# Where the inverse square roots of twelve normalisations are computed: eleven VectorE instructions or one GpSimd power

## The chip, the cores and the metric

The kernel runs on one core of a Trainium2 chip. The core has five engines, each with an instruction queue of its own that it works through strictly in order: TensorE (PE in the profile; PEld is its weight load), VectorE (DVE), ScalarE (ACT), GpSimd (POOL) and SyncE (SP, which here only starts DMAs). Engines wait for each other through semaphores. The metric is the device time of one execution in microseconds (us), the median of several runs; less is better.

## What is computed

Two transformer layers on `x` of 2 x 512 tokens with 256 features. What matters here are the normalisations, each of which needs `1/sqrt(v)` of a few numbers for every token:

```
def rmsnorm(x, w, eps=1e-05):
    return x * rsqrt(mean(x * x, axis=-1) + eps) * w
...
# layer 0: layer norm, then an RMS norm of it, feed a gated linear attention (GLA)
S = S * exp(gt) + kt * vt            # 512 steps, a scan over the tokens
ot = einsum('bhk,bhkd->bhd', qt, S)
o = (o - mean(o)) * rsqrt(var(o) + 1e-05)   # per token and head, 16 heads
x = x + (silu(g) * o) @ Wo
x = x + (silu(xn2 @ W1) * (xn2 @ W3)) @ W2  # xn2 = rmsnorm(x): a SwiGLU MLP
# beside it, a ternary-weight MLP on the layer-normed x
h = silu(gate) * up;  h = h * rsqrt(mean(h * h) + eps);  y = h @ Wp
# layer 1: softmax attention, then rmsnorm, a router and a mixture of 8 experts
```

## The kernel before, in words

The tokens are two chunks `c` = 0, 1 of 512 tokens; a chunk is four tiles (TPC = 4) of 128 tokens on the 128 partitions. So the inverse roots of one chunk are a block of 128 partitions x 4 numbers (`ff`, `rms`, `xm`), x 8 (`norm`, `ln`: two norms at once) or x 64 (`gn`: 4 tiles x 16 heads). They all live in the small tile `small`.

The twelve places, in order of time: `norm` of chunk 0 and 1 (prologue), `ff` 0 (norm of the ternary MLP's hidden row), `gn` 0 (norm of the GLA output), `rms` 0, `ff` 1, `gn` 1, `rms` 1, `ln` 0, `ln` 1 (layer 1's first norms) and `xm` 0, `xm` 1 (norm ahead of the router). In the kernel before, all are made by VectorE in `rsqrt`: `rsqrt_guess` (L1529, L1530: a shift and a subtraction on the number's bits) and three Newton rounds (L1535, L1536, L1538), eleven instructions, each waiting for the one before through `link`.

Each engine runs the same written-out list of steps, `order_of(engine)`: a PROLOGUE, then steps put into numbered slots, sorted by slot and by a rank within the slot, then ORDER. A step of which an engine has no part is skipped by it. LATE moves a kind of step one slot later on one engine; RANK says which kinds come first in a slot, and what is not in RANK comes last in the order in which it was put. Slots 0 to 31 carry the 32 GLA steps: PE replicates (`rep`), DVE multiplies (`upd`, L1690) and scans (`scan`, L1698), POOL multiplies with q (`read`, L2192), PE sums (`red`). Between them lie the ternary MLP (`in`, `hm` (DVE L1670; POOL sums the squares into `acc`, L2182), `out`), the group norm of chunk 0 in four stages (`gn`, c, 0 to 3) and its projection (`got`, `wo`). From slot 35 the SwiGLU MLP runs (`hm`: DVE L1670, ACT `ah`, POOL `al` L2174), and beside it the group norm of chunk 1 and the splitting of the next weights in POOL (`w`: `w3l`, `w2l`; `qkvw`). Then come the layer-1 projections, the softmax attention over 64 heads (DVE takes row maxima, L1828) and the experts.

The consumers of the inverse roots: `ff_out` adds the ternary MLP's result to `X` (L1681) and so frees the PSUM banks that PE's `out` of the other chunk waits for; `group_norm` stage 3 scales `cen` (L1730); `rms_scale` (L1750) and `ln2_rows` (L1761) scale `XA`; `norm_rows` (L1577 on DVE, L2159 on POOL) normalises `X`.

Of the kernel before, what the change touches and what calls it, by code (L numbers as in the profile page):

```python
# [30 lines left out]
P = 128  # L31
# [17 lines left out]
RSQRT_SEED = float(0x5F3759DF)  # L49
# [57 lines left out]
def build(nc, orders, w_pack, t_pack, c_pack, r_pack, e_pack, vec_pack, bias_pack, x_in, out):  # L107
    from contextlib import ExitStack
    ctx = ExitStack()
    with ctx:  # L110
# [58 lines left out]
        ah_at = mlp_at + (2 + 3) * CH * 4  # L169
        QSX = at("QSX", [6, CH], F32, ah_at)  # L170
# [149 lines left out]
        factors = tally("norm_factors")  # L320
# [22 lines left out]
        sqr = tally("hidden_square")  # L343
        accr = tally("square_sum")
# [105 lines left out]
        PROLOGUE += [("z", 0), ("norm", 1, "guess")] + pj(0, 3) + [("e1", 0), ("norm", 1, "newton")] + low_at(0, 3) + pj(0, 4)  # L450
# [45 lines left out]
        put(22, ("ss", 0))  # L496
        put(34, ("ss", 1))
# [11 lines left out]
        for n in range(4):  # L509
# [6 lines left out]
        put(32, ("rms", 0, 0))  # L516
# [5 lines left out]
                [("wo", 1, 0)], [("wo", 1, 1)], [("rms", 1, 0)], [("xat", 1, 0)], [("xat", 1, 1)],  # L522
# [5 lines left out]
        for i, s in enumerate(SWS):  # L528
# [7 lines left out]
        LATE = {"PE": {}, "ACT": {"hm": 1}, "POOL": {"hm": 1, "read": 1},  # L536
                "DVE": {"upd": 1, "scan": 1, "tern": 1, "hm": 1, "tr": 1, "proj": 1, "otok": 1, "wo": 1, "ss": 1, "got": 1, "xat": 1}}
        RANK = {"PE": ("rep", "in", "tern", "red", "out"), "ACT": ("in", "hm", "ternA"),
                "POOL": ("read", "tern", "hm"), "DVE": ("tern0", "hm", "upd", "tern", "scan")}
# [261 lines left out]
        def _(pe):  # L801
# [713 lines left out]
        def _(dve):  # L1515
# [11 lines left out]
            def rsqrt_guess(y_, v, n, tmp):  # L1527
                t_ = small[:, tmp, 0:n]
                link(nc.vector.tensor_single_scalar(t_.bitcast(I32), v.bitcast(I32), 1, ALU.logical_shift_right))  # L1529
                link(nc.vector.tensor_scalar(y_.bitcast(I32), t_.bitcast(I32), -1.0, RSQRT_SEED, ALU.mult, ALU.add))  # L1530

            def newton(y_, v, n, tmp, times, told_by=None):
                t_ = small[:, tmp, 0:n]
                for i in range(times):
                    link(nc.vector.scalar_tensor_tensor(t_, y_, -0.5, v, ALU.mult, ALU.mult))  # L1535
                    link(nc.vector.tensor_tensor(t_, t_, y_, ALU.mult))  # L1536
                    last = told_by if told_by and i == times - 1 else link
                    last(nc.vector.scalar_tensor_tensor(y_, t_, 1.5, y_, ALU.add, ALU.mult))  # L1538
# [14 lines left out]
            def norm_stats(layer, c, part=None):  # L1553
# [3 lines left out]
                v, r = small[:, 0, 0:2 * TPC], small[:, 1, 0:2 * TPC]  # L1557
# [7 lines left out]
                if part is None:  # L1565
                    newton(r, v, 2 * TPC, 4, 2)
                elif part == "newton":
                    newton(r, v, 2 * TPC, 4, 2, lambda ins: ins.then_inc(*factors.tick(c)))
                    dve.wait_ge(*factors.upto(c))

            def norm_rows(layer, c):
                r1, r2 = small[:, 1, 0:TPC], small[:, 1, TPC:2 * TPC]
                rows = [("xt", XN, r1), ("x1", XA, r2)]
                for v, dst, r in (rows if layer == 1 else rows[::-1]):
# [131 lines left out]
            def group_norm(c, stage):  # L1706
# [16 lines left out]
                elif stage == 1:  # L1723
                    dve.wait_ge(*g_sq.upto(c))
                    link(nc.vector.tensor_reduce(sm.rearrange("p (t h) -> p t h", h=H), byh(L0["otok"]), AX.X, ALU.add))
                    link(nc.vector.tensor_scalar(vr, sm, 1.0 / HD, EPS, ALU.mult, ALU.add))
                elif stage == 2:
                    rsqrt(rs_, vr, 64, 4)
                else:
# [6 lines left out]
            def rms_factors(half):  # L1736

                v, r = small[:, 0, 0:TPC], small[:, 1, 0:TPC]
                if half == 1:
                    link(nc.vector.tensor_tensor(v, mv[:, :, 0], mv[:, :, 0], ALU.mult))  # L1740
                    link(nc.vector.scalar_tensor_tensor(v, v, EPS, mv[:, :, 1], ALU.add, ALU.add))
                    rsqrt_guess(r, v, TPC, 4)
                    newton(r, v, TPC, 4, 1)
                else:
# [643 lines left out]
```

## Time and profile before

| | us |
|---|---|
| median of 3 runs | 693.27 |
| the three runs | 693.71, 693.27, 685.2 |
| span of the profiled execution (first to last instruction) | 690.8 |
| time of that execution itself | not listed apart; the median run is 2.47 above the span |
| busy: PE, DVE, ACT, POOL | 569.0, 495.7, 302.9, 216.2 |
| GpSimd instructions | 225 |

The span is shorter than a run because a run also holds what lies before the first and after the last instruction. Busy time is an average over stages with different limits, so it does not say which engine a stage waits for.

### The profile page before, as it was taken

Reading aid. Unit: us, or ns where it says so; the run is one execution under the profiler, and the core shown is the slowest. Engines: PE = TensorE matmul, PEld = TensorE weight load, DVE = VectorE, ACT = ScalarE, POOL = GpSimd, SP = SyncE. Lnnn points to the kernel's source line nnn. Section 1 sums busy time; section 2 is a strip of 40 time slices with the busy share of each in tenths; the row PEclk is TensorE's granted clock in tenths of the full one; section 3 lists DMA queues with packets and bytes.
Section 4 is the critical chain, followed back from the end, with each engine's and each line's share of the span. In section 5 each row is a group of like instructions: output and inputs, shape, how many; then the busy total and the mean of one; then the engine's idle time right before and its main releaser. Section 6 shows DMA issues by size and latency. Waiting matters only on the chain.

```text
span 690.8 us, 10947 instructions
## 1 busy us (share of the span) xinstructions
PE 569.0 (82%) x3674; PEld 407.0 (59%) x3678; DVE 495.7 (72%) x1078; ACT 302.9 (44%) x554; POOL 216.2 (31%) x225
## 2 busy tenths in 40 slices
PE   2677689679577799997599988988978889999990
PEld 1544357468356588883255554454535478888870
DVE  5799976997795576858488778768771467767753
ACT  1645433213221223552266545544535656666640
POOL 2765556436545223665200010010044011121120
PEclk9889999989789899996599999999988999999995
DMA  6122000000321004599873431500025794000005
GB/s 185 61 87 75 29 0 1 1 0 1 87 62 30 2 1 133 94 222 284 148 126 69 87 70 24 95 2 2 2 67 234 263 371 138 23 25 32 24 32 190
DMA packets 32733, 58.36 MB, mean 84 GB/s; under 512 B 6822, under 2 KB 24646, under 8 KB 30118
## 3 DMA queue, kind: packets, MB, share of 16 engines
q1 hardware_dynamic: 30422, 52.32, 28.1%
q0 software_dynamic: 1872, 5.13, 2.1%
q8 instruction: 31, 0.51, 0.3%
q10 hardware_dynamic: 384, 0.20, 0.1%
q14 instruction: 24, 0.20, 0.1%
HBM read 41.84 MB, written 15.51 MB: 83 GB/s over the span
## 4 chain that ended last, share of the span: by engine, by line
PE 40%; DVE 11%; issue 3%; POOL 2%; ACT 2%; DMA 1%; SPq 0%; ACTq 0%; POOLq 0%; DVEq 0%
PE bank L823 19%; DVE small L1828 5%; PE bank L1087 5%; PE bank L1064 4%; PE bank L1037 4%; PE bank L817 4%; PE bank L1039 2%; PE bank L1066 1%; DMA yt<-results 1%; PE bank L1104 1%; POOL P3c L2259 1%; POOL rt L2203 1%; ACT PTa L1367 1%; DVE XA L1857 1%; POOL P L2259 1%
## 5 line engine op out<-in xcount | busy, mean ns | idle before, releaser
L1828 DVE TENSOR_REDUCE small<-bank 128x1 f32<-128x256 f32 (+3 forms) x256 | 107.5, 482 | 15.4 <-PE bank L1039 14.2
L1037 PE MATMUL bank<-Ks,Qs 96*128 96x256 bf16 (+3 forms) x256 | 66.6, 327 | 8.6 <-DVE small L1828 7.0
L2104 DVE TENSOR_TENSOR wl<-wall,wh 128x1024 fp32r<-128x1024 f32 x46 | 56.2, 1222 | 22.3 <-ACT wh L1496 21.0
L1064 PE MATMUL bank<-Qs,Ks 99*128 99x512 bf16 (+3 forms) x256 | 60.3, 312 | 8.2 <-issue 7.8
L1367 ACT ACTIVATE PTa<-bank 128x512 f32<-128x512 f32 (+1 forms) x96 | 43.5, 530 | 34.9 <-PE bank L1066 27.2
L1367 ACT ACTIVATE PTb<-bank 128x512 f32<-128x512 f32 (+1 forms) x96 | 43.9, 530 | 27.9 <-PE bank L1066 27.4
L1064 PEld LDWEIGHTS bank<-Qs,Ks 99*128 99x128 bf16 x256 | 25.7, 100 | 51.1 <-issue 32.1
L1039 PE MATMUL bank<-maskb,identb 128*128 128x128 bf16 x256 | 55.4, 234 | 0.0
L1318 ACT ACTIVATE sg<-bank 128x512 f32<-128x512 f32 (+1 forms) x28 | 16.7, 597 | 75.3 <-PE bank L823 75.3
L1496 ACT CAST wh<-wall 128x1024 fp32r x46 | 48.0, 1044 | 2.0 <-issue 0.9
L1066 PE MATMUL bank<-identb,maskb 128*128 128x128 bf16 x256 | 48.2, 226 | 0.0
L2192 POOL TENSOR_TENSOR QSX<-QT,S 128x512 f32<-128x512 f32 x24 | 31.3, 1304 | 41.8 <-DVE S L1698 38.9
L823 PE MATMUL bank<-wall,hT 128*128 x184 | 43.5, 379 | 0.8 <-ACT hT L1511 0.8
L2266 POOL TENSOR_TENSOR X<-X,XA 128x1024 f32<-128x1024 f32 x2 | 4.7, 2366 | 122.3 <-DVE XA L1868 122.3
L1037 PEld LDWEIGHTS bank<-Ks,Qs 96*128 96x128 bf16 x256 | 25.9, 103 | 28.7 <-DVE small L1828 22.4
L1698 DVE TENSOR_TENSOR_SCAN S<-AT,bank 128x512 f32<-128x512 f32 x32 | 38.9, 1215 | 0.6
L823 PEld LDWEIGHTS bank<-wall,hT 128*128 128x128 f32 x184 | 34.7, 189 | 6.3 <-issue 1.0
L823 PE MATMUL bank<-wh,xh 128*128 128x512 f32 x92 | 38.2, 415 | 0.0
L823 PE MATMUL bank<-wpr,hm 128*128 128x256 f32 x128 | 32.5, 399 | 6.6 <-DVE X L1681 6.6
L823 PE MATMUL bank<-wl,xh 128*128 128x512 f32 x92 | 36.2, 393 | 0.0
L823 PE MATMUL bank<-wh,xl 128*128 128x512 f32 x92 | 35.8, 389 | 0.0
L1670 DVE TENSOR_TENSOR hm<-sg,bank 128x512 f32<-128x512 f32 (+1 forms) x28 | 19.1, 682 | 21.6 <-PE bank L823 21.3
(363 smaller groups left out, 1531.7 us busy)
## 6 DMA issues: line engine op xcount, KB each, us to landing
wall<-e_pack SPq DMA_DIRECT2D x8, 1536.0 KB, 8.6
Qs<-pieces SPq DMA_DIRECT2D x48, 128.0 KB, 5.8
stg<-w_pack SPq DMA_DIRECT2D x18, 256.0 KB, 2.8
pieces<-P SPq DMA_DIRECT2D x9, 512.0 KB, 8.5
wf<-t_pack SPq DMA_DIRECT2D x12, 256.0 KB, 2.7
Ks<-pieces SPq DMA_DIRECT2D x8, 384.0 KB, 5.2
sorted_rows<-blank SPq DMA_DIRECT2D x1, 2944.0 KB, 12.7
Ks<-pieces SPq DMA_DIRECT2D x8, 256.0 KB, 4.5
```

The costliest lines, as they stand in the source:

```text
L823: last = nc.tensor.matmul(outap, a, b_, start=start and i == 0, stop=stop and i == n - 1, **kw)
L1037: nc.tensor.matmul(banks[b][:, o:o + w], Q[0:96, h, i * P:(i + 1) * P], K[0:96, h, 0:w], start=True, stop=False)
L1039: last = nc.tensor.matmul(banks[b][:, o + w - P:o + w], identb[:], maskb[:], start=False, stop=True)
L1064: nc.tensor.matmul(banks[b][:, o:o + w], K[0:99, h, j * P:(j + 1) * P], Q[0:99, h, j * P:CH], start=True, stop=False)
L1066: last = nc.tensor.matmul(banks[b][:, o:o + P], maskb[:], identb[:], start=False, stop=True)
L1087: last = nc.tensor.matmul(banks[6][32 * hh:32 * hh + 17, j * P:CH], L1[f"Va{a}"][:, c * TPC + j, 4 * (q % 4) + hh, :], pt[:, hh, PT_AT[j]: ...
L1367: nc.scalar.activation(pt[:, g % 4, lo_:lo_ + w], banks[b][:, 0:w], ACT.Exp).then_inc(*ex.tick((g, i_)))
L1496: nc.scalar.copy(weight_part("h", i, half), wall[:, bass.ds(place + half * KC * EI, KC * EI)])\
L1698: nc.vector.tensor_tensor_scan(L0["S"][:, i % 2, :], L0["AT"][:, c * CH:(c + 1) * CH], banks[i % 2][:], 0.0, ALU.mult, ALU.add).then_inc(* ...
L1828: last = nc.vector.tensor_reduce(mxv[:, i, h:h + 1], banks[b][:, o:o + w], AX.X, ALU.max, negate=True)
L2104: nc.vector.tensor_tensor(weight_part("l", i, half), wall[:, bass.ds(place + half * KC * EI, KC * EI)], weight_part("h", i, half).bitcast( ...
L2192: nc.gpsimd.tensor_tensor(readout(i), L0["QT"][:, c * CH:(c + 1) * CH], L0["S"][:, i % 2, :], ALU.mult).then_inc(*qs.tick(i))
```

## The change

Each of the twelve rounds of eleven VectorE instructions is taken out. VectorE writes the variance and signals it (`var`); GpSimd raises it to the power -0.5 with one two-input instruction, whose second input is one constant read again for every element (`minus_half`), and signals that (`inv`); whoever uses the root waits for `inv`. For `ff` 0, `ff` 1 and `rms` 0, VectorE's variance step gets the rank `first`, so that it comes ahead of the other steps of its slot, and the use stays at the end of the slot. (`gn`, c, 2), once VectorE's eleven instructions, is now GpSimd's power alone. For `norm` 0 of the prologue GpSimd makes the power ahead of its first weight split, for chunk 1 ahead of its `norm_rows`.

```diff
-        put(22, ("ss", 0))
-        put(34, ("ss", 1))
+        put(22, ("ss", 0), ("ssx", 0))
+        put(34, ("ss", 1), ("ssx", 1))
...
-        put(32, ("rms", 0, 0))
+        put(32, ("rms", 0, 0), ("rms", 0, 1))
...
-        LATE = {"PE": {}, "ACT": {"hm": 1}, "POOL": {"hm": 1, "read": 1},
+        LATE = {"PE": {}, "ACT": {"hm": 1}, "POOL": {"hm": 1, "read": 1, "ss": 1},
...
+                if engine == "DVE" and slot < SW_AT and (op == "ss" or it == ("rms", 0, 0)):
+                    op = "first"
...
-            def rsqrt(y_, v, n, tmp):
-
-                rsqrt_guess(y_, v, n, tmp)
-                newton(y_, v, n, tmp, 3)
...
                 if part in (None, "guess"):
                     tell(nc.vector.tensor_scalar(v[:, 0:TPC], mv[:, :, 1], EPS, None, ALU.add))
-                    link(nc.vector.tensor_scalar(v[:, TPC:2 * TPC], mv[:, :, 1], 1.0 + EPS, EPS * EPS, ALU.mult, ALU.add))
-                    rsqrt_guess(r, v, 2 * TPC, 4)
-                    newton(r, v, 2 * TPC, 4, 1)
...
+                    nc.vector.tensor_scalar(v[:, TPC:2 * TPC], mv[:, :, 1], 1.0 + EPS, EPS * EPS, ALU.mult, ALU.add)\
+                        .then_inc(*var.tick(("norm", layer, c)))
...
+            def ff_squares(c):
+                dve.wait_ge(*mm.upto(("ss", c)))
+                nc.vector.tensor_scalar(small[:, 0, 0:TPC], banks[3][:, 0:TPC], 1.0 / 1024, EPS_F32, ALU.mult, ALU.add)\
+                    .then_inc(*var.tick(("ff", c)))
+                dve.wait_ge(*var.upto(("ff", c)))
+
             def ff_out(c):
...
+                dve.wait_ge(*inv.upto(("ff", c)))
...
-                elif stage == 2:
-                    rsqrt(rs_, vr, 64, 4)
-                else:
+                    nc.vector.tensor_scalar(vr, sm, 1.0 / HD, EPS, ALU.mult, ALU.add).then_inc(*var.tick(("gn", c)))
+                    dve.wait_ge(*var.upto(("gn", c)))
+                elif stage == 3:
+                    dve.wait_ge(*inv.upto(("gn", c)))
...
+            nc.gpsimd.memset(minus_half, -0.5).then_inc(*pool_chain.tick(pool_chain.n))
...
+            def inverse_roots(key, dst, src, n):
+
+                pool.wait_ge(*var.upto(key))
+                nc.gpsimd.tensor_tensor(small[:, dst, 0:n], small[:, src, 0:n], minus_half.broadcast_to([P, n]), ALU.pow)\
+                    .then_inc(*inv.tick(key))
+
+            inverse_roots(("norm", 0, 0), 1, 0, 2 * TPC)
...
+                elif op == "ss":
+                    inverse_roots(("ff", it[1]), 1, 0, TPC)
+                elif op == "gn" and it[2] == 2:
+                    inverse_roots(("gn", it[1]), 8, 7, 64)
+                elif op == "rms" and it[2] == 0:
+                    inverse_roots(("rms", it[1]), 1, 0, TPC)
+                elif op == "xm" and it[2] == 1:
+                    inverse_roots(("xm", it[1]), 1, 0, TPC)
+                elif op == "ln" and it[2] == 0:
+                    inverse_roots(("norm", 1, it[1]), 1, 0, 2 * TPC)
```

## Rows read from the trace of the kernel before

**Rows 1.** Windows: stretch, its length, busy PE PEld DVE ACT POOL, PE clock, DMA, GB/s.
```profile
126.00:156.00 30.00, 20.55 (x87) 15.05 (x85) 28.86 (x47) 6.55 (x11) 11.40 (x8) 0.89 0.00 1
156.00:176.00 20.00, 19.89 (x111) 15.41 (x109) 14.78 (x19) 6.84 (x13) 14.96 (x13) 1.00 0.06 15
200.00:225.00 25.00, 17.77 (x101) 15.17 (x102) 17.43 (x26) 6.56 (x11) 12.60 (x12) 0.93 0.08 22
262.00:285.00 23.00, 22.62 (x149) 20.05 (x148) 16.67 (x47) 9.21 (x20) 9.52 (x16) 1.00 0.65 148
```

**Rows 2.** Chain that ended last, attention: start, length, what.
```profile
420.00 1.58 DVE rows L1761 x4
423.94 0.63 PE bank L817 x4
```

**Rows 3.** VectorE's timeline: start, length, line, operation, tiles.
```profile
134.70 1.18 DVE L1535 SCALAR_TENSOR_TENSOR small<-small 128x4 f32<-128x4 f32 x1
...
137.49 1.66 DVE L1681 SCALAR_TENSOR_TENSOR X<-bank,small,X 128x256 f32<-128x256 f32 x4
...
150.98 1.20 DVE L1730 TENSOR_TENSOR cen<-cen,small 128x1024 f32<-128x1024 f32 x1
...
183.92 1.14 DVE L1750 TENSOR_SCALAR cen<-XA,small 128x256 f32<-128x256 f32 x4
...
195.36 1.66 DVE L1681 SCALAR_TENSOR_TENSOR X<-bank,small,X 128x256 f32<-128x256 f32 x4
...
212.22 1.23 DVE L1730 TENSOR_TENSOR cen<-cen,small 128x1024 f32<-128x1024 f32 x1
...
227.59 0.17 DVE L1529 TENSOR_SCALAR small<-small 128x4 int32<-128x4 int32 x1
...
229.77 1.14 DVE L1750 TENSOR_SCALAR cen<-XA,small 128x256 f32<-128x256 f32 x4
...
413.71 0.17 DVE L1529 TENSOR_SCALAR small<-small 128x4 int32<-128x4 int32 x1
...
414.71 1.68 DVE L1828 TENSOR_REDUCE small<-bank 128x1 f32<-128x256 f32 x4
...
417.48 0.18 DVE L1839 CAST mtok<-small 128x16 bf16<-128x16 f32 x1
```

**Rows 4.** GpSimd's timeline: start, length, line, operation, tiles, idle before.
```profile
27.82 4.84 POOL L2159 TENSOR_SCALAR XA<-X,mv,small 128x256 f32<-128x256 f32 x4 [4.82 <-DVE small L1538]
...
134.60 1.26 POOL L2182 TENSOR_TENSOR acc<-acc,sq 128x512 f32<-128x512 f32 x1
...
145.57 1.26 POOL L2182 TENSOR_TENSOR acc<-acc,sq 128x512 f32<-128x512 f32 x1 [0.47 <-ACT sq L1331]
...
180.88 1.00 POOL L2132 TENSOR_TENSOR w3l<-stg,w3h 128x384 fp32r<-128x384 f32 x1
188.88 3.77 POOL L2132 TENSOR_TENSOR w2l<-stg,w2h 128x512 fp32r<-128x512 f32 x3 [6.99 <-ACT w2h L1410]
...
207.02 1.30 POOL L2174 TENSOR_TENSOR al<-hm,ah 128x512 fp32r<-128x512 f32 x1
```

**Rows 5.** VectorE's timeline of the prologue: the last Newton instruction ahead of GpSimd's `norm_rows`.
```profile
27.54 0.17 DVE L1538 SCALAR_TENSOR_TENSOR small<-small 128x8 f32<-128x8 f32 x1
```

**Rows 6.** GpSimd's groups by line and shape: busy us, mean ns of one, idle before.
```profile
L2203 POOL TENSOR_TENSOR rt<-qkt,rope 128x64 f32<-128x64 f32 x16 | 4.4, 294 | 0.0
...
L2142 POOL TENSOR_TENSOR wo1l<-stg,wo1h 128x512 fp32r<-128x512 f32 x1 | 1.3, 1261 | 0.1
...
L2142 POOL TENSOR_TENSOR wrl<-stg,wrh 128x256 fp32r<-128x256 f32 x1 | 0.7, 722 | 0.1
...
L2275 POOL TENSOR_SCALAR rows<-share 128x8 f32<-128x8 f32 x1 | 0.2, 210 | 7.2 <-DMA sorted_rows<-rows,slot_i 7.2
```

**Rows 7.** Waits of the first 36 us: who, for whom, us in total, times, longest.
```profile
PEld bank L817 <- DMA bias<-bias_pack: 10.7, 1, 10.7
```

**Rows 8.** ScalarE's timeline, end of the prologue.
```profile
31.95 0.61 ACT L1309 ACTIVATE ab<-wf 128x512 bf16<-128x512 f32 x1
```

More of the change, by code:

```diff
@@ L169, in build @@
         ah_at = mlp_at + (2 + 3) * CH * 4
+        minus_half = small[:, 11, 63:64]
         QSX = at("QSX", [6, CH], F32, ah_at)
@@ L534, in build @@
         put(SW_AT + SWO_AT[2], ("l1", 0, "xt", 0), ("l1", 0, "xt", 1))
-        LATE = {"PE": {}, "ACT": {"hm": 1}, "POOL": {"hm": 1, "read": 1},
-                "DVE": {"upd": 1, "scan": 1, "tern": 1, "hm": 1, "tr": 1, "proj": 1, "otok": 1, "wo": 1, "ss": 1, "got": 1, "xat": 1}}
+        LATE = {"PE": {}, "ACT": {"hm": 1}, "POOL": {"hm": 1, "read": 1, "ss": 1},
+                "DVE": {"upd": 1, "scan": 1, "tern": 1, "hm": 1, "tr": 1, "proj": 1, "otok": 1, "wo": 1, "ss": 1, "ssx": 1, "got": 1, "xat": 1}}
         RANK = {"PE": ("rep", "in", "tern", "red", "out"), "ACT": ("in", "hm", "ternA"),
-                "POOL": ("read", "tern", "hm"), "DVE": ("tern0", "hm", "upd", "tern", "scan")}
+                "POOL": ("read", "tern", "hm"), "DVE": ("first", "tern0", "hm", "upd", "tern", "scan")}
         def order_of(engine):
@@ L1525, in link @@
                 told()
[L1527 to L1538, printed above, removed]
-            def rsqrt(y_, v, n, tmp):
-                rsqrt_guess(y_, v, n, tmp)
-                newton(y_, v, n, tmp, 3)
             def stats(src, c):
@@ L1556, in norm_stats @@
                     stats(X, c)
-                v, r = small[:, 0, 0:2 * TPC], small[:, 1, 0:2 * TPC]
+                v = small[:, 0, 0:2 * TPC]
                 if part in (None, "guess"):
                     tell(nc.vector.tensor_scalar(v[:, 0:TPC], mv[:, :, 1], EPS, None, ALU.add))
-                    link(nc.vector.tensor_scalar(v[:, TPC:2 * TPC], mv[:, :, 1], 1.0 + EPS, EPS * EPS, ALU.mult, ALU.add))
-                    rsqrt_guess(r, v, 2 * TPC, 4)
-                    newton(r, v, 2 * TPC, 4, 1)
[L1565 to L1569, printed above, removed]
+                    nc.vector.tensor_scalar(v[:, TPC:2 * TPC], mv[:, :, 1], 1.0 + EPS, EPS * EPS, ALU.mult, ALU.add)\
+                        .then_inc(*var.tick(("norm", layer, c)))
             def norm_rows(layer, c):
@@ L1573, in norm_rows @@
                 rows = [("xt", XN, r1), ("x1", XA, r2)]
+                dve.wait_ge(*inv.upto(("norm", layer, c)))
                 for v, dst, r in (rows if layer == 1 else rows[::-1]):
@@ L1734, in group_norm, with rms_squares @@
                         .then_inc(*tok.tick(("got", c)))
[L1736 to L1744, printed above, removed]
-                    newton(r, v, TPC, 4, 2)
+            def rms_squares(key):
+                v = small[:, 0, 0:TPC]
+                link(nc.vector.tensor_tensor(v, mv[:, :, 0], mv[:, :, 0], ALU.mult))
+                nc.vector.scalar_tensor_tensor(v, v, EPS, mv[:, :, 1], ALU.add, ALU.add).then_inc(*var.tick(key))
+                dve.wait_ge(*var.upto(key))
             def rms_scale(c, dst, key):
                 r = small[:, 1, 0:TPC]
+                dve.wait_ge(*inv.upto(("rms", c)))
                 for t in range(TPC):
@@ L2001, in _ @@
                 elif op == "ss":
+                    ff_squares(it[1])
+                elif op == "ssx":
                     ff_out(it[1])
@@ L2020, in _ @@
                 elif op == "rms":
-                    for pr in range(2):
-                        dve.wait_ge(*dproj.upto(("wo", it[1], pr)))
-                    rms_rows(it[1], L0["cen"], "xat")
+                    c = it[1]
+                    if it[2] == 0:
+                        for pr in range(2):
+                            dve.wait_ge(*dproj.upto(("wo", c, pr)))
+                        stats(XA, c)
+                        rms_squares(("rms", c))
+                    else:
+                        rms_scale(c, L0["cen"], "xat")
                 elif op == "swout":
@@ L2154, in norm_rows @@
                 r1, r2 = small[:, 1, 0:TPC], small[:, 1, TPC:2 * TPC]
-                pool.wait_ge(*factors.upto(c))
+                inverse_roots(("norm", 0, c), 1, 0, 2 * TPC)
+                pool.wait_ge(*inv.upto(("norm", 0, c)))
                 for v, dst, r in (("x1", XA, r2), ("xt", XN, r1)):
```

30 lines of the change are left out of this document (11 added, 19 removed).

## The prediction, made before the change was run

> **What bounds the kernel now.** I read the windows by stage first, because the busy shares of the whole span mix stages with different limits. From 126 to 156 us VectorE is busy 28.86 of 30 us while PE idles 9.45; from 156 to 176 PE is busy 19.89 of 20; from 200 to 225 neither is full (PE 17.77, VectorE 17.43 of 25), so a chain through both sets the pace; from 262 to 285 PE is full again (22.62 of 23) [rows 1]. So a microsecond saved on VectorE counts where PE waits for it and is worth nothing where PE is full, but once won ahead of a full stretch it is kept: PE simply starts that stretch earlier. The chain that ended last can be followed back only to 279.9 us; in the attention it passes through VectorE around the `xm` norms (L1761 at 420.00, then PE at 423.94) [rows 2]. For everything before, I went through VectorE's and GpSimd's timelines place by place.
>
> **What is removed.** In the quietest place, `rms` 1, eleven instructions last from 227.59 to 229.77, 2.18 us, so twelve places hold at least 26 us of VectorE's queue. Five places hold more, because VectorE's tiny instructions are held up while GpSimd works: the 128x4 L1535 at 134.70 takes 1.18 us, beside a 128x512 `acc` of GpSimd that starts at 134.60 and takes 1.26 [rows 3, 4]. A removed 0.17 us instruction can thus give back over 1 us. Yet the root is not gone, it is queued on another in-order engine, and its user waits for it. What is won at a place is therefore the old start of the user minus the new end of the power, and that hangs on what stands ahead of the power in GpSimd's list.
>
> **What is added: hop and power.** A semaphore from VectorE to GpSimd costs about 0.11 us: the last Newton instruction ends at 27.71, `norm_rows` of GpSimd starts at 27.82 [rows 4, 5]. I take 0.1 each way. No power runs in the trace of before. Bound from below: a two-input GpSimd instruction, 0.294 us for 64 columns, 0.21 us for 8 (one input) [rows 6]. Bound from above, unless the power is done in some other way than arithmetic on whole columns (the slow rival below): as much as the eleven steps would cost as eleven GpSimd instructions, 11 x 0.294 = 3.2 us for 64 columns and 11 x 0.21 = 2.3 us for 4 or 8. It cannot cost less than nothing, as it must read and write. Between them I take one instruction's start and eleven passes' slope: from 256 to 512 columns a two-input instruction grows by 0.539 us, 2.1 ns a column [rows 6], leaving a start of 0.18; so 0.18 + 64 x 11 x 2.1 ns = 1.7 us for 64 columns, 0.35 for 8 and 0.27 for 4. This lies nearer to the lower row, since one instruction has one start.
>
> No page of the Trainium skill that I found has a price for the power; "GPSIMD Engine Reference", section 3.1, gives about 12 cycles per element for data-dependent branching at 1.2 GHz, by which 64 columns would be an estimated 0.64 us above the start, and the sum below some 2 us larger. Its section 4.1 says to keep elementwise work on VectorE, which speaks against the change; it weighs instruction against instruction, and here one stands against eleven.
>
> **Place by place.**
>
> `ff` 0: the variance moves to the start of its slot, so it is ready long before; but GpSimd's list has `read` and `acc` ahead of the power, and `read` waits for the scan of the same slot. `acc` ended at 134.60 + 1.26 = 135.86; 0.2 later through the moved variance step, plus 0.27 and 0.1, the root is there at 136.4. The user started at 137.49 [rows 3, 4]. Won: 1.1 of a round that took over 4 us. PE's `out` of chunk 1 waits for exactly this user.
>
> `gn` 0: again `read` and `acc` go first; `acc` ended at 146.83 [rows 4], now 1.1 earlier; plus 1.7 and 0.1 the root is there at 147.5, against a user at 150.98 [rows 3]. Won: 3.5 in all, the 1.1 of `ff` 0 included. In between VectorE goes on with the next slot's multiply, update and scan. Behind the power on GpSimd waits the next `read`; the scan after next needs it, a slot later. Then PE's full stretch (156 to 176) starts 3.5 earlier.
>
> `rms` 0: statistics and variance now go ahead of the last update and scan, which they delay by some 2 us; the power stands behind the last `read` and the last `w3l`, which ended at 181.88. Plus 0.27 and 0.1 this is 182.25, against 183.92 [rows 3, 4]: 1.7, of which I take 1.5, as `read` may come later with the delayed scan.
>
> `ff` 1: no VectorE step lies between variance and use, so VectorE stands still; what it waits for is three `w2l` splits, ended at 192.65. Plus 0.27 and 0.1: 193.0 against 195.36 [rows 3, 4]. Won 2.4.
>
> `gn` 1: the power stands behind `al`, ended at 208.32. Plus 1.7 and 0.1: 210.1 against 212.22 [rows 3, 4]. Won 2.1, and PE waits for this user.
>
> `rms` 1: GpSimd is free; a weight split that now stands behind the power has its use only in the layer-1 projections. 2.18 minus 0.47 gives 1.7.
>
> `xm` 0 and 1: the power is needed two heads later and is hidden; its cover is the row maxima (the four at 414.71 take 1.68). From 413.71 to 417.48 the removed steps and these maxima take 3.77, so 2.1 leave VectorE, which stands on the chain [rows 2, 3]. I take 2.0 each, 4.0, the rest lost where PE becomes the next to be late. If the cover were too short, at most this would be lost.
>
> `norm` 0: VectorE saves 2.2 less 0.55, but PE's first instruction also waited for a DMA until 10.7 us [rows 7]. I take nothing; 0.8 at most. `norm` 1: its rows feed GpSimd earlier, but VectorE next waits for ScalarE, which reaches its first `ab` at 31.95 after a gapless run of its own [rows 8]. Nothing; 1 at most. `ln` 0 and 1: PE is full there [rows 1]. Nothing; 1 at most. The GpSimd constant is written while GpSimd waits for its first weights: nothing.
>
> The sum: 3.5 + 1.5 + 2.4 + 2.1 + 1.7 + 4.0 = 15.2 us. The profiled span of 690.8 becomes 675.6; with the 2.5 us by which the median run lies above that span, 678 us, 2.2% less. At the lower price of the power the two `gn` win 1.4 more each: 18.0, 675. At the upper price (3.2 and 2.3) `gn` 0 with `ff` 0 wins about 0, `rms` 0 loses 0.5, `ff` 1 wins 0.4, `gn` 1 0.6, `rms` 1 loses 0.3, `xm` 4.0: about 4, 689.
>
> **The rivals.** (1) The power is slow per column. If a column costs as much as a small GpSimd instruction, 0.21 us [rows 6], 64 columns take 13.4 us; two such (a logarithm and an exponential) 26.9. Each microsecond on the 64-column power costs about 2.4 us in all (two `gn` places on the path, and the sixteenth part of it at the smaller places). The gain is used up at 8 us, and over 2% is lost from 13.8 us on. At 13.4 the time is 706, at 26.9 it is 738; midway 722. For it: a power is no adder's work. Against: nothing in the trace shows GpSimd working one element at a time, its 128x8 and 128x64 instructions are cheap. (2) The wait takes the place of the work: in the GLA and SwiGLU stretch the user is held by GpSimd's queue as late as before, for instance because `read` and `acc` are themselves late, and only `rms` 1 and `xm` remain: 5.7 won, 688. The 1.1 of 4 us at `ff` 0 speaks for it, `gn` 1 against it. (3) More is won: PE's waits in 126 to 156 and 200 to 225 come with clocks of 0.89 and 0.93 [rows 1]; if shorter waits keep the clock up and GpSimd and VectorE cease to hold each other up, another 10 of the 16.7 us that PE idles there go: 668. (4) The first power alone is slow. The start waits for it, so that each microsecond over the 2.2 of the round it replaces delays everything; with 4.84 us, the longest run of four GpSimd instructions in the rows [rows 4], 3 are lost: 681. "GPSIMD Engine Reference", section 2.1, tells of some 6 us at the first call of a freshly loaded GpSimd routine, by which it would be 4, 682; no run here shows that the power is such a routine, and GpSimd's other operations show no slow first call. That the change does not do what it says I exclude: the eleven instructions leave the program.
>
> **How the numbers follow.** Forecast 678 (675 to 689 by the price bounds): 0.50. Rivals: (1) 0.17, (2) 0.15, (3) 0.12, (4) 0.06. Two per cent, about what a measurement of this kernel can tell from no change, is 13.9 us: 679.4 and 707.1. Of the forecast's 0.50, 0.33 lie below 679.4. Faster: 0.33 + 0.12 = 0.45. Slower: most of (1), 0.13. Same: 0.17 + 0.15 + 0.06 + 0.04 = 0.42. The range runs from 667, so that (3) is in, to 696, with (1) left out.
>
> **What would show it.** The price: the length of the power in GpSimd's rows, 128x64 against 128x4, and the distance to its user on VectorE. `ff` 0 and `ff` 1: VectorE idle ahead of L1681, the wait ended by GpSimd, about 3 and 4 us. `gn`: the power directly behind `acc` and `al`. `xm`: no wait at all, and PE's transposes 2 us earlier. The forecast is wrong if the power of 64 columns takes over 3.2 us, if a wait for GpSimd is as long as the removed round, or if the start of the span moves.

## The result and the profile after

The changed kernel takes 702.07 us (median of 4 runs, 697.42 to 705.0), the kernel before in the same comparison 689.24 (685.04 to 693.71): ratio 1.0175, interval 1.0129 to 1.0221. The forecast was 678; the time lies outside the range, in the first rival's direction. The profiled execution took 699.76 us, its span 698.0, 7.2 longer than the span before; the executions of the two kernels lie up to 7.6 and 8.7 us apart, so the medians (12.8 us) say more than two single profiles.

VectorE lost 30.6 us of work (495.7 to 465.1 us, 1078 to 946 instructions), as planned. The price of the power stands in one group of GpSimd's rows:

```profile
L2136 POOL TENSOR_TENSOR small<-small 128x4 f32<-128x4 f32 (+2 forms) x12 | 33.8, 2820 | 29.6 <-DVE small L1723 15.6
```

33.8 us for twelve. The two 128x64 ones are far from the mean; here they are on GpSimd's timeline at `gn` 0 and `gn` 1 (start, duration):

```profile
144.70 1.27 POOL L2174 TENSOR_TENSOR acc<-acc,sq 128x512 f32<-128x512 f32 x1 [1.06 <-ACT sq L1334]
145.93 10.55 POOL L2136 TENSOR_TENSOR small<-small 128x64 f32<-128x64 f32 x1
156.44 1.27 POOL L2184 TENSOR_TENSOR QS<-QT,S 128x512 f32<-128x512 f32 x1
...
214.09 1.29 POOL L2166 TENSOR_TENSOR al<-hm,ah 128x512 fp32r<-128x512 f32 x1
215.34 10.52 POOL L2136 TENSOR_TENSOR small<-small 128x64 f32<-128x64 f32 x1
```

The shapes average 10.54 us (64 columns), 1.66 (8) and 1.02 (4). From 8 to 64 columns that is (10.54 - 1.66) / 56 = 158 ns a column, over a start of about 0.39 us. The powers stand where the prediction put them, directly behind `acc` and `al` [rows 4]. VectorE's waits for them, from the waits of the changed kernel (total, times, longest):

```profile
DVE cen L1713 <- POOL small L2136: 22.5, 2, 12.9
DVE X L1664 <- POOL small L2136: 8.5, 2, 4.9
DVE cen L1730 <- POOL small L2136: 4.5, 2, 3.3
```

And VectorE's timeline at the users that stand in [rows 3] for before (in brackets the idle time ahead):

```profile
136.03 1.66 DVE L1664 SCALAR_TENSOR_TENSOR X<-bank,small,X 128x256 f32<-128x256 f32 x4 [3.59 <-POOL small L2136]
...
156.51 2.27 DVE L1713 TENSOR_TENSOR cen<-cen,small 128x1024 f32<-128x1024 f32 x1 [9.51 <-POOL small L2136]
...
202.39 1.66 DVE L1664 SCALAR_TENSOR_TENSOR X<-bank,small,X 128x256 f32<-128x256 f32 x4 [4.94 <-POOL small L2136]
...
225.90 1.63 DVE L1713 TENSOR_TENSOR cen<-cen,small 128x1024 f32<-128x1024 f32 x1 [12.95 <-POOL small L2136]
```

`ff` 0 comes 1.5 us earlier than before, `gn` 0 5.5 later, `gn` 1 13.7 later. Of the 1.5 us only 0.4 are won at the place itself: the `cen` row of the group norm ahead of it is already 1.0 us earlier. First the row before the change, then after it:

```profile
129.46 1.22 DVE L1720 TENSOR_TENSOR cen<-otok,small 128x1024 f32<-128x1024 f32 x1
```

```profile
128.43 1.23 DVE L1703 TENSOR_TENSOR cen<-otok,small 128x1024 f32<-128x1024 f32 x1
```

The windows show what the late users do to PE (per engine the busy time and count; then PE's granted clock), to be held against [rows 1]:

```profile
126.00:156.00 30.00, 19.11 (x79) 13.99 (x77) 14.91 (x20) 6.08 (x10) 17.98 (x8) 0.84 0.00 1
156.00:176.00 20.00, 14.37 (x60) 10.23 (x61) 14.26 (x15) 4.51 (x8) 10.97 (x9) 0.73 0.00 1
...
200.00:225.00 25.00, 14.70 (x75) 11.73 (x73) 9.89 (x13) 4.37 (x7) 18.20 (x10) 0.91 0.18 52
```

The stretch from 156 to 176, in which PE was full before, now has PE idle for 5.6 of 20 us, and VectorE's 28.86 busy of 30 ahead of it have become 14.91. VectorE waits for GpSimd, and PE, through VectorE, with it.

### The profile page after: what moved, and what is told of

Its sections match the earlier page's. It is cut to its first block, busy times and chain, and to the rows that moved or that the text cites. A ratio compares the mean times of both kernels' runs of the same rounds, so it can differ in the third digit from the quotient of the medians.

```text
span 698.0 us, 10835 instructions
## 1 busy us (share of the span) xinstructions
PE 566.1 (81%) x3678; PEld 405.4 (58%) x3678; DVE 465.1 (67%) x946; ACT 302.5 (43%) x554; POOL 250.3 (36%) x238
## 4 chain that ended last, share of the span: by engine, by line
PE 37%; DVE 9%; DMA 4%; ACT 3%; POOL 2%; issue 2%; SPq 1%; ACTq 0%; POOLq 0%; DVEq 0%
PE bank L826 19%; PE bank L1090 4%; PE bank L820 4%; DVE small L1802 4%; PE bank L1067 4%; PE bank L1040 3%; DMA Qs<-mT 2%; PE bank L1069 1%; DMA pieces<-P 1%; PE bank L1042 1%; DMA yt<-results 1%; ACT PTa L1370 1%; SPq L721 1%; PE bank L1107 1%; POOL P3c L2261 1%
## 5 line engine op out<-in xcount | busy, mean ns | idle before, releaser
L1802 DVE TENSOR_REDUCE small<-bank 128x1 f32<-128x256 f32 (+3 forms) x256 | 107.7, 483 | 14.6 <-PE bank L1042 13.7
L2136 POOL TENSOR_TENSOR small<-small 128x4 f32<-128x4 f32 (+2 forms) x12 | 33.8, 2820 | 29.6 <-DVE small L1723 15.6
L826 PE MATMUL bank<-XTh,wgu 128*128 128x512 f32 x64 | 27.1, 424 | 12.6 <-DVE hm L1650 10.5
## 6 DMA issues: line engine op xcount, KB each, us to landing
pieces<-P SPq DMA_DIRECT2D x9, 512.0 KB, 10.2
```

The costliest lines, as they stand in the source:

```text
L826: last = nc.tensor.matmul(outap, a, b_, start=start and i == 0, stop=stop and i == n - 1, **kw)
L1802: last = nc.vector.tensor_reduce(mxv[:, i, h:h + 1], banks[b][:, o:o + w], AX.X, ALU.max, negate=True)
L2136: nc.gpsimd.tensor_tensor(small[:, dst, 0:n], small[:, src, 0:n], minus_half.broadcast_to([P, n]), ALU.pow)\
```

## The experiments

The theory after reading both traces: the two 64-column powers cost the time, by VectorE's standing still; the ten small powers win about what was forecast. The rivals: the way through GpSimd's queue costs, not the price; or what was saved at the small places lay beside other work. Each variant was executed 6 or 12 times beside the kernel before; `e3`, `e4` and `e5` leave roots out and serve for their time only.

| run | median us | ratio to before (95%) |
|---|---|---|
| `e1_gn_back` | 681.08 | 0.9877 (0.9834 to 0.9921) |
| `e2_gn_only` | 706.97 | 1.0263 (1.0219 to 1.0307) |
| `e3_gn_mult` | 675.06 | 0.9769 (0.9732 to 0.9806) |
| `e4_all_mult` | 670.87 | 0.9716 (0.9679 to 0.9754) |
| `e5_gn_half` | 691.87 | 1.0021 (0.9990 to 1.0053) |
| `e6_gn_xm_back` | 686.31 | 0.9963 (0.9932 to 0.9994) |
| `e7_gn_blocked` | 684.18 | 0.9921 (0.9887 to 0.9956) |
| `e8_gn_delay` | 700.60 | 1.0166 (1.0123 to 1.0209) |
| `e9_roots_first` | 675.15 | 0.9767 (0.9712 to 0.9823) |
| `e10_gn_on_gpsimd_by_newton` | 687.42 | 0.9977 (0.9942 to 1.0013) |

Before stood at 690.0 beside the first four, 689.6 beside the next four, 690.8 beside the last two.

**`e1_gn_back`: one part undone.**

```diff
-                    .then_inc(*var.tick(("gn", c)))       # and the wait for inv
+                    rsqrt(rs_, vr, 64, 4)                 # stage 2, VectorE
...
-                    inverse_roots(("gn", it[1]), 8, 7, 64)
```

> The changed kernel with one part undone: the two 64-column roots of the group norm are made by VectorE again (guess and three Newton rounds); the ten small roots of 4 and 8 columns stay with GpSimd. Theory (the price of the 64-column power): the small powers alone win, by the traces, 1.5 at ff 0, 1.7 at ff 1, about 1 and 1.5 at the two rms, up to 4 at the two xm, so the kernel is 7 to 10 us faster than before (about 681) and about 20 us faster than the changed kernel. Rival (queue: a root that goes to GpSimd and back costs more than the round it replaces, whatever its length): the small ones lose as well, each of six on the path some 1 us; the kernel is 2 to 6 us slower than before, 7 to 11 faster than the changed one. Rival (cover: only VectorE work that nobody waits for was saved at the small places): equal to before within 2 us.

8.9 us faster than before (5.5 to 11.5 by the interval), about 21 faster than the changed kernel: the theory, within its numbers. The small powers are worth having.

**`e2_gn_only`: the other part alone**, the same lines of the change in the kernel before.

> The kernel before with the other part alone: only the two 64-column roots of the group norm go to GpSimd as one power each; all small roots stay with VectorE. Theory (price): the users come some 7 us later at each of the two places (7.0 and 6.7 in the traces after the small gains are taken off), and PE's clock falls a little more; 14 to 18 us slower than before, 703 to 707, and so 2 to 6 slower than the changed kernel. Rival (queue): the two places cost a queue wait only, 3 to 5 us, about 693. Rival (cover): as the theory, but equal to the changed kernel within 2 us.

17.0 us slower than before: the theory. The two parts (-8.9 and +17.0) add up to +8, against the 12.8 that was measured for both together; the three intervals of about 3 us each leave room for the difference.

**`e3_gn_mult` and `e4_all_mult`: the price alone**, all waits and places kept.

```diff
-small[:, src, 0:n], minus_half.broadcast_to([P, n]), ALU.pow)
+small[:, src, 0:n], minus_half.broadcast_to([P, n]), ALU.mult if n == 64 else ALU.pow)   # e3
+small[:, src, 0:n], minus_half.broadcast_to([P, n]), ALU.mult)                           # e4
```

> The changed kernel with the power of the two 64-column instructions replaced by a multiplication: same engine, same place in GpSimd's list, same waits and semaphores, same shape; only the operation is another, so the group norm's root is left out and its rows are scaled by other numbers. Theory (price): the instruction takes 0.3 us in place of 10.5, each of the two waits of VectorE for it falls from 9.5 and 13.0 to under 3 us, and the time falls by 18 to 24 us from the changed kernel, to 678 to 684, below the kernel before by 6 to 11. Rival (queue): the waits stay above 7 us, the time falls by under 6 us.

> The changed kernel with all twelve powers replaced by multiplications, same places and waits: no root is made anywhere, so every normalisation scales by other numbers. It gives the best that the move could have won if the power cost no more than the cheapest GpSimd instruction. Theory (price): by the place-by-place sum with the low price, 18 us below the kernel before, that is 671; by what the traces after show at the small places, 3 to 4 us less than the variant with only the two large powers cheap, so 674 to 680. Rival (cover: at the small places nothing more is won since the waits end by other work): equal to the variant with only the two large powers cheap, within 2 us.

With nothing but the operation exchanged, the 27 us between 702.07 and 675.06 are gone, 3 more than the 18 to 24 that I had expected. The second input, one constant read again, is the same in the multiplication, so it is the power that is dear and not that reading. VectorE's timeline of `e3_gn_mult` and GpSimd's row ahead of the second user:

```profile
147.41 1.20 DVE L1713 TENSOR_TENSOR cen<-cen,small 128x1024 f32<-128x1024 f32 x1
...
203.07 1.63 DVE L1713 TENSOR_TENSOR cen<-cen,small 128x1024 f32<-128x1024 f32 x1 [2.72 <-POOL small L2136]
```

```profile
201.51 1.28 POOL L2166 TENSOR_TENSOR al<-hm,ah 128x512 fp32r<-128x512 f32 x1
202.75 0.28 POOL L2136 TENSOR_TENSOR small<-small 128x64 f32<-128x64 f32 x1
```

At `gn` 0 no wait is left. That the user comes at 147.41, next to the 147.5 at which the prediction had put the root, is luck: 147.5 holds a price of 1.7, the root of `e3` is there at 146.66, and VectorE takes the user up only when its own scan ahead of it is done.

`e4`, with all powers cheap, takes 670.87: 19.1 us below the kernel before (17.0 to 22.1 by the interval), where the prediction's sum with the lowest price of the `gn` power had 18.0. Against `e3` it is 4.2 us (by the two ratios 3.7, with an uncertainty of 3.6), so the time alone does not exclude the rival that equals `e3` within 2 us. The rows do: from the user of `rms` 0 to that of `ff` 1 `e4` takes 8.99 us and `e3` 9.79, and the difference is that of the one instruction (0.20 for 1.01). That a root which goes through GpSimd's queue costs more than the round it replaces, whatever its length, is refuted by `e1`, `e3` and `e4`.

**`e5_gn_half`: half the price.**

```diff
+nc.gpsimd.tensor_tensor(small[:, 8, 32:64], small[:, 7, 32:64], minus_half.broadcast_to([P, 32]), ALU.mult)
-inverse_roots(("gn", it[1]), 8, 7, 64)
+inverse_roots(("gn", c_), 8, 7, 32)
```

> The changed kernel with the power of the group norm made for 32 of the 64 columns only, the other 32 by a multiplication just ahead of it on GpSimd (half of the group norm's roots are left out). By the measured 158 ns a column the pair takes 5.5 + 0.25 us in place of 10.5. Theory (each microsecond of GpSimd's time at the two places costs the kernel its double, and in addition some 3.5 us after each place, where PE runs at a lower clock): between 0.3 us (675) and 10.5 us (702) it lies on the straight line, 2.64 us for each, at 689. Rival (double only, the rest comes with long waits): 686. Rival (a threshold: nothing is lost as long as the wait is shorter than the removed round of 4 to 6 us): 675 to 680.

691.87: the straight line's 689 lies at the lower end of the interval, the two other cases outside. By the medians the first 5.4 us of price (0.3 to 5.7) cost 16.8 us and the next 4.8 cost 10.2. That is 3.1 and 2.1 us for each microsecond of the power, with uncertainties of some 0.6 and 0.8: by the times it can be a fixed part that comes with the wait and then one microsecond at each of the two places, or the straight line's 2.64 throughout. The markers on VectorE, one profile each, speak for the fixed part (start of the user, us):

| | `gn` 0 | `rms` 0 | `ff` 1 | `gn` 1 | `rms` 1 |
|---|---|---|---|---|---|
| before | 150.98 | 183.92 | 195.36 | 212.22 | 229.77 |
| `e1_gn_back` | 148.98 | 181.59 | 191.39 | 208.22 | 223.19 |
| `e3_gn_mult` (0.3 us) | 147.41 | 179.99 | 189.78 | 203.07 | 219.36 |
| `e4_all_mult` (0.3, small ones 0.2) | 145.10 | 176.90 | 185.89 | 199.17 | 214.69 |
| `e5_gn_half` (5.7) | 150.82 | 187.29 | 197.09 | 215.69 | 233.82 |
| changed (10.5) | 156.51 | 192.59 | 202.39 | 225.90 | 244.72 |
| `e7_gn_blocked` | 150.49 | 182.55 | 192.35 | 207.78 | 229.70 |
| `e8_gn_delay` | 158.56 | 191.97 | 201.76 | 225.62 | 243.18 |

From `gn` 0 to `rms` 0, where no 64-column power runs, `e3` takes 32.58 us, `e5` 36.47 and the changed kernel 36.08; from `gn` 1 to `rms` 1 16.29, 18.13 and 18.82. Together 5.7 us with half the price and 6.0 with the whole.

**`e7_gn_blocked` and `e8_gn_delay`: who has to wait?** One keeps GpSimd's queue blocked and lets VectorE go on, the other keeps VectorE back and leaves the queue free.

```diff
-inverse_roots(("gn", it[1]), 8, 7, 64)
+inverse_roots(("gn", it[1]), 3, 7, 64)        # e7: a row that nobody reads; VectorE: rsqrt(rs_, vr, 64, 4)
...
+newton(rs_, vr, 64, 4, (10, 9)[c])            # e8: on e1, ahead of the scaling of cen
```

> The changed kernel with the two 64-column powers left where they are on GpSimd, but written to a row that nobody reads: VectorE makes the group norm's root itself (guess and three Newton rounds) and does not wait for GpSimd. GpSimd's queue is blocked for 10.5 us twice, and what stands behind the power there (the next read of the GLA, the next low part of the SwiGLU) is as late as in the changed kernel. Theory (VectorE's wait is what costs): close to the variant without these powers, 681 to 686. Rival (the blocked queue costs as much: read and low part come 10 us later): 695 to 702.

> The variant with the group norm's roots back on VectorE (681), with ten and nine more Newton rounds ahead of the group norm's scaling, each of three instructions of some 0.26 us: VectorE's user comes 7.8 and 7.0 us later, about as late as in the changed kernel, but no power runs and GpSimd's queue is free. Theory (VectorE's wait is what costs, and PE's lower clock after it): 681 + 14.8 + about 7 = 700 to 704. Rival (the blocked queue of GpSimd makes the part beyond the direct delay): 681 + 14.8 = 694 to 697.

`e7` is 684.18: with the power running, but nobody waiting for it, most of the loss is gone. Nor does the power slow VectorE. The Newton steps and both `cen` instructions of `gn` 1 run at their usual length, though the power occupies GpSimd from 205.29 to 215.82 (a row of GpSimd, four of VectorE, one of PE):

```profile
205.29 10.53 POOL L2155 TENSOR_TENSOR small<-small 128x64 f32<-128x64 f32 x1
```

```profile
207.52 0.23 DVE L1541 SCALAR_TENSOR_TENSOR small<-small 128x64 f32<-128x64 f32 x1
207.78 1.23 DVE L1732 TENSOR_TENSOR cen<-cen,small 128x1024 f32<-128x1024 f32 x1
209.04 1.22 DVE L1735 TENSOR_TENSOR cen<-cen,XA 128x1024 f32<-128x1024 f32 x1
...
224.07 0.69 DVE L2013 TENSOR_TENSOR XA<-bank,rows 128x512 f32<-128x512 f32 x1 [10.15 <-PE bank L827]
```

```profile
219.03 0.58 PE L827 MATMUL bank<-w2h,ah 128*128 128x256 f32 x1 [4.83 <-POOL al L2185]
```

The last two rows are the blocked queue's share: `al` stands behind the power, PE waits 4.83 us for `al` and VectorE 10.15 for PE, and from `gn` 1 to `rms` 1 `e7` takes 21.92 us against 14.97 in `e1`. Ahead of `gn` 1 it wins 1.4 (15.43 us from `ff` 1 against 16.83), and at `gn` 0 the queue costs nothing (32.06 against 32.61). By the medians `e7` is 3.1 us slower than `e1`, with an uncertainty of some 4.

`e8` came to 700.60, inside the theory's 700 to 704, but not by the theory's parts: the nineteen rounds delayed the users by 9.6 and 7.0 us more than `e1`, and the two stretches behind them lost 0.8 and 2.6, not the 7 that I had written. With these delays the rival's sum would be 681 + 16.6 = 697.7, which `e8`'s interval (698.1 to 704.0) does not exclude once that of `e1` (3 us either way) is added. So `e8` does not decide between the two, and it is `e7` that speaks against the rival.

So where does the part behind `gn` 0 come from (36.08 in place of 32.58)? It falls wholly within the 13 us after the user. VectorE's rows of the changed kernel behind the user at 156.51, then those of `e3_gn_mult` behind the user at 147.41:

```profile
158.81 2.17 DVE L1716 TENSOR_TENSOR cen<-cen,XA 128x1024 f32<-128x1024 f32 x1
160.91 0.67 DVE L1650 TENSOR_TENSOR hm<-sg,bank 128x512 f32<-128x512 f32 x1
...
165.07 1.22 DVE L1681 TENSOR_TENSOR_SCAN S<-AT,bank 128x512 f32<-128x512 f32 x1
169.28 0.69 DVE L1567 TENSOR_TENSOR X1l<-bank,X1h 128x512 fp32r<-128x512 f32 x1 [2.98 <-ACT X1h L1280]
```

```profile
150.74 0.68 DVE L1650 TENSOR_TENSOR hm<-sg,bank 128x512 f32<-128x512 f32 x1
...
154.49 1.22 DVE L1681 TENSOR_TENSOR_SCAN S<-AT,bank 128x512 f32<-128x512 f32 x1
...
156.68 0.69 DVE L1567 TENSOR_TENSOR X1l<-bank,X1h 128x512 fp32r<-128x512 f32 x1 [0.97 <-ACT X1h L1280]
```

From the user to `hm` it is 4.40 us against 3.33: the power ends, and the `read` behind it (156.44) starts together with VectorE's user, which takes 2.27 beside it and not 1.20. From `hm` to the second scan 4.16 against 3.75; from there to `X1l`, which waits for ScalarE's `X1h` and so for PE's transposes, 4.21 against 2.19. These 1.07, 0.41 and 2.02 are the 3.50. For the last, the windows and PE's rows of the changed kernel:

```profile
156.50:161.00 4.50, 0.00 (x0) 0.00 (x0) 4.46 (x3) 0.00 (x0) 3.40 (x2) 0.50 0.00 0
161.00:165.10 4.10, 3.47 (x12) 1.36 (x12) 3.73 (x6) 0.63 (x1) 1.58 (x2) 0.50 0.00 0
165.10:169.10 4.00, 4.00 (x19) 3.06 (x16) 1.20 (x1) 0.44 (x1) 2.19 (x2) 0.77 0.00 0
```

```profile
150.72 0.39 PE L826 MATMUL bank<-XTl,wgu 128*128 128x512 f32 x1
161.63 0.80 PE L826 MATMUL bank<-XTh,wgu 128*128 128x512 f32 x1 [10.53 <-DVE hm L1650]
162.23 0.63 PE L826 MATMUL bank<-XTl,wgu 128*128 128x512 f32 x1
...
163.64 1.94 PE L992 MATMUL bank<-QSX,selt 128*32 128x512 f32 x8
```

PE has stood still for 10.5 us and comes back at the lower of its two clocks (0.50 is 1.2 GHz): a product takes 0.63 us in place of 0.39, the eight of `red` 1.94. In the same place of `e3_gn_mult` the granted clock is 1.00 throughout, and the eight take 1.07. `e8_gn_delay` has the clock without the power: PE comes back at 0.50 after 10.6 us, the user takes its usual 1.23, and of the three parts only the two of PE's clock are there (4.17 and 3.52, against 3.75 and 2.19; the last is shorter than in the changed kernel, and the clock is back sooner, 0.94 in place of 0.77 from 165.1 to 169.1). `e5_gn_half` shows 0.50 as well, after 5.6 us of idle PE, which agrees with a part that does not grow with the price. Behind `gn` 1 it is the same in the changed kernel: after 11.6 us without work PE is at 0.50 from 226 to 234 and takes 1.97 us for eight transposes, where `e3` (1.00 from 203 to 219.4) takes 1.09, and VectorE's user is as long in both (1.63):

```profile
229.79 1.97 PE L820 MATMUL bank<-ident,cen 128*128 128x128 f32 x8 [11.62 <-DVE cen L1716]
```

The low clock as such is nothing new: in the kernel before PE comes back the same way at `ff` 0, at 0.51 from 139.2 to 143.3, and its first eight products take twice their later 1.89 us:

```profile
139.29 3.75 PE L823 MATMUL bank<-wpr,hm 128*128 128x256 f32 x8 [6.63 <-DVE X L1681]
```

These are readings of the rows; no run kept PE busy through the wait at `gn`.

**`e6_gn_xm_back`: the attention's two roots.**

```diff
-                        rms_squares(("xm", c))
...
+                        rsqrt_guess(r, v, TPC, 4)
+                        newton(r, v, TPC, 4, 1)    # two more rounds in stage 2
```

> The variant with the group norm's roots back on VectorE, and in addition the roots of the two xm norms (in the attention) back on VectorE; only ff, rms, norm and ln stay with GpSimd. Prediction's step: xm is worth 2.0 us each, so it is 4 us slower than the variant with only the group norm back (681), 685. Rival (hidden: VectorE's xm round lies beside PE's work in the attention, the 5.5 us by which the attention's profile was shorter after the change is scatter): 681, within 1.5 us.

686.31, 5.2 us above `e1`; by the two ratios 0.0086 of before, 5.9 us, with an uncertainty of some 3.6. The prediction's 4 is inside, the hidden rival's 1.5 just outside. The rows decide it. From the first `xm` row of a chunk to the scaling of its rows VectorE takes 6.6 us in the kernel before and 4.5 after the change, without a wait for the power; chunk 0, before and after:

```profile
413.33 0.15 DVE L1740 TENSOR_TENSOR small<-mv 128x4 f32<-128x4 f32 x1
...
419.92 1.66 DVE L1761 SCALAR_TENSOR_TENSOR rows<-XA,small,route 128x256 f32<-128x256 f32 x4
```

```profile
430.22 0.15 DVE L1722 TENSOR_TENSOR small<-mv 128x4 f32<-128x4 f32 x1
...
434.76 1.67 DVE L1742 SCALAR_TENSOR_TENSOR rows<-XA,small,route 128x256 f32<-128x256 f32 x4
```

In either chunk it is 6.6 to 6.8 us in the three kernels with Newton there (before, `e2`, `e6`) and 4.5 in the nine that have GpSimd's instruction. The gain stays: up to the CAST after the next row maxima (L1839 before) it is 17.4 to 17.6 us against 15.3 to 15.4. So each chunk wins 2.0.

**`e9_roots_first`: price or place, at the small powers?**

```diff
+if engine in ("DVE", "POOL") and slot < SW_AT and (op == "ss" or it == ("rms", 0, 0)):
+    op = "first"              # on e1: also in GpSimd's list
+if engine == "POOL" and it == ("ss", 1):
+    late = 0                  # ahead of the three w2l
```

> The variant with the group norm's roots back on VectorE (681), and the small powers of ff 0, ff 1 and rms 0 put first in GpSimd's slot, ahead of read, acc and the weight splits (ff 1 ahead of the three w2l). In that variant VectorE stands still for 3.6, 4.9 and 3.3 us at these places, while one power takes 1.0. Theory (of these waits only the power and a hop are the price, the rest is the place in GpSimd's list): waits fall to some 1.3 us, 2.3 + 3.7 + 2.1 = 8 us are won, of which a part is lost as read and splits come a microsecond later; 673 to 677. Rival (the splits and reads moved back are needed as soon): 680 to 684.

675.15, the theory: the waits of VectorE at `ff` 0, `ff` 1 and `rms` 0 fall from 3.6, 4.9 and 3.3 us to nothing, 1.2 and 0.3. This version is faster than the kernel before by 2.3% (1.8 to 2.9) and than the changed one by some 27 us; against `e1` it is 5.9 us by the medians, 7.6 by the ratios with an uncertainty of 5. Part of the gain is lost again: VectorE takes 1.0 us more from `ff` 1 to `gn` 1 and 1.6 more from `gn` 1 to `rms` 1 than in `e1`, and PE's low clock is gone behind `ff` 0 (1.00 from 133.4 to 140) but stands behind PE's next wait, of 3.0 us (0.50 from 144 to 148).

**`e10_gn_on_gpsimd_by_newton`: the same engine without the power**, the guess by VectorE, then on GpSimd:

```diff
+for i in range(3):
+    step(nc.gpsimd.tensor_tensor(t_, y_, v_, ALU.mult))
+    step(nc.gpsimd.tensor_tensor(t_, t_, y_, ALU.mult))
+    step(nc.gpsimd.tensor_scalar(t_, t_, -0.5, 1.5, ALU.mult, ALU.add))
+    ins = nc.gpsimd.tensor_tensor(y_, t_, y_, ALU.mult)
+    if i < 2:
+        step(ins)
```

> The changed kernel with the group norm's roots made on GpSimd by Newton too, in place of the power: VectorE makes the integer guess, GpSimd twelve instructions of 64 columns in a chain (three rounds of four). Same place in GpSimd's list and same wait of VectorE; by the 0.29 us of one such instruction and some 0.05 us between them about 4.1 us in place of 10.5. It is the way that the prediction's upper price stood for. Theory (doubly what GpSimd takes, and a fixed part after each wait): between the half power (5.7 us, 692) and the multiplication (0.3 us, 675), 688 to 690; so no faster than before. Rival (a power is the only thing that is dear, arithmetic on GpSimd is as good as on VectorE): 681, as with VectorE's Newton.

687.42, half a microsecond below the theory's 688 to 690 and far from the rival's 681. Twelve instructions of 0.24 to 0.33 us take 4.55 us, from 145.84 to 150.39; one power takes 10.5.

## Why the prediction was wrong, step by step

**The step that failed** is the price: "Bound from above ... 11 x 0.294 = 3.2 us for 64 columns", and the value of 1.7 taken from it. It measured 10.54, three times the bound and six times the value. The bound counted what a Newton root would cost on GpSimd, and that was not far off (4.5 us in `e10`); it says nothing about an operation that is done in another way. The sentence had left one case open, that the power is done in some other way than arithmetic on whole columns, and by its price that is the case; how it is done the runs do not show. The small powers were mis-sized as well: 1.02 and 1.66 us against 0.27 and 0.35, inside their bounds of 2.3.

The Trainium skill, "GPSIMD Engine Reference", section 3.1, gives about 12 cycles an element for data-dependent branching; by it I had estimated 0.64 us for 64 columns above the start. The rows give 10.1, 16 times as much, and the measurement decides. The advice in the Trainium skill, "GPSIMD Engine Reference", section 4.1, to keep elementwise work on VectorE comes out right here for the two places of 64 columns (`e1` against the changed kernel) and not for the ten small ones taken together (`e1` against the kernel before).

**Rival (1)** was the case. It put a column at 0.21 us (measured 0.158) and the total slope at 2.4 us for each microsecond of the large power. By its own formula 10.54 us give 678 + 2.4 x (10.54 - 1.7) = 699 us, against 702.07; between `e3` and the changed kernel the slope is 2.6. It had a chance of 0.17 and was left out of the range, which went to 696. I held against it that GpSimd's 128x8 and 128x64 instructions are cheap; these rows were additions and multiplications, so they were no evidence about a power.

**The sum.** With the measured prices put into the prediction's places, 15.2 - 2 x 8.8 - 4 x 0.75 = -5.4. Two terms come on top that the prediction had at nothing. One is the 6.0 us behind the two waits: PE at the lower clock, and at `gn` 0 VectorE beside `read`. The other is 1.4 us at `rms` 1. There the prediction saw that a weight split would follow the power and asked only when the split is needed; but the split now runs beside VectorE's user, which takes 2.51 us in place of 1.14. GpSimd's rows and VectorE's in the changed kernel, and VectorE's next row before, behind the 229.77 of [rows 3]:

```profile
244.59 0.62 POOL L2121 TENSOR_SCALAR qkv0h<-stg 128x512 fp32r<-128x512 f32 x1
245.30 1.26 POOL L2123 TENSOR_TENSOR qkv0l<-stg,qkv0h 128x512 fp32r<-128x512 f32 x1
```

```profile
244.72 2.51 DVE L1730 TENSOR_SCALAR cen<-XA,small 128x256 f32<-128x256 f32 x4 [1.20 <-POOL small L2136]
247.16 0.67 DVE L1650 TENSOR_TENSOR hm<-sg,bank 96x512 f32<-96x512 f32 x1
```

```profile
230.82 0.68 DVE L1670 TENSOR_TENSOR hm<-sg,bank 96x512 f32<-96x512 f32 x1
```

-5.4 - 6.0 - 1.4 = -12.8 is the loss by the medians (8.9 to 15.2 us by the interval); that it fits to the tenth is luck. The rows say the same: from the `cen` ahead of `ff` 0 to the `hm` behind `rms` 1 it is 101.4 us before (129.46 to 230.82) and 118.7 after (128.43 to 247.16), and of these 17.4 us the two `xm` give back 4.1. The two spans differ by 7.2 only, since the profiled execution was some 3 us above its median before and 2.3 below it after; behind the last `xm` place, where the code is the same, the twelve profiles take between 197.6 and 203.8 us. The prediction's 2.5 us from span to median had the same weakness: an execution lies 1.8 us above its own span, and the later medians of the kernel before, 689 to 691, are not above the 690.8 of its profiled span.

**Place by place.** Each value is what is won against the kernel before from one user's start to the next (`ff` 0 and `gn` 0 from the `cen` ahead of `ff` 0, so that `gn` 0 includes `ff` 0); the forecast is that of the lowest price of the `gn` power, which `e4` comes nearest to.

| | forecast, lowest price | `e4` | changed |
|---|---|---|---|
| `ff` 0 | 1.1 | 1.3 | 0.4 |
| `gn` 0 with `ff` 0 | 4.9 | 4.0 | -6.6 |
| `rms` 0 | 1.5 | 1.1 | -3.1 |
| `ff` 1 | 2.4 | 2.5 | 1.6 |
| `gn` 1 | 3.5 | 3.6 | -6.7 |
| `rms` 1 | 1.7 | 2.0 | -1.3 |
| `xm`, both | 4.0 | 4.1 | 4.1 |

So with cheap powers the accounting by places holds to 1 us at each (the 1.4 us by which `rms` 1's user is longer is not in these starts), and what failed is the price and what a long wait brings with it. At `rms` 0 of the changed kernel 3.5 of the loss is the part behind `gn` 0. In `e1`, with no long wait, `rms` 0 wins 0.3.

**The other rivals.** (2), the wait in place of the work, happens at `rms` 0 and nearly at `ff` 0, where VectorE waits 3.3 and 3.6 us and 0.3 and 0.4 are won; `e9` shows that these waits are GpSimd's order and not the power. (3), more won by the clock, has its mirror image here: behind the longer waits PE's clock was lower. (4) falls: the first power, at 7.25 us, takes 1.67, like the three later ones of 8 columns (1.64 to 1.67).

## What to carry to other kernels

An operation that does not appear in the trace has no upper bound from operations that do: run it once by itself, at the size in question, before the sum is made, and where that can't be done keep the slow case inside the range. When work is moved to another in-order engine, price it by the waiting time of its user, which is the operation's length plus what stands ahead of it in the other queue: here the first was 10.5 us and decided against the 64 columns, and the second was 3 to 4 us at each of three places and could be taken away by a change of rank. Then look at what the queue does next: an instruction that follows can run beside the user and lengthen it, as at `gn` 0 and `rms` 1. The same operation can be right for 4 columns and wrong for 64; decide by place.

## What the runs showed of the hardware that was not expected

- The power costs GpSimd 158 ns for each column of 128 partitions, over a start of about 0.39 us; a multiplication of the same 64 columns by the same constant takes 0.28 to 0.30 us.
- GpSimd's 128x512 instructions hold VectorE's up, its power does not. Beside `read` a 128x1024 `cen` takes 2.27 us and not 1.20; under the 10.5 us power, 1.23. The Trainium skill, "GPSIMD Engine Reference", section 1 (Specifications), tells of contention with VectorE instructions that have two SBUF inputs (or use a mode with two ports); the first row agrees, and the second shows that not every GpSimd instruction with two inputs does it.
- After 3.0 us (`e9`), 5.6 us (`e5`) and 10.5 us (changed) without work PE came back at a granted clock of 0.50, and products behind it took 1.6 to 1.9 times as long; behind `gn` 0 this went with 2.8 us on top of the shorter wait (0.42 + 2.39) and 2.4 on top of the longer one (0.41 + 2.02), so no more for the long wait than for the short.
